# First layer: the row maxima of two heads at once, on the two row halves of the matrix array

## The reference

```python
k_rope = _rotary_apply(c_kv @ W_k_rope, cos, sin)          # 32 rows, shared by all 16 heads
k = (c_kv @ W_k_up).reshape(Bb, Tt, NH, HD)                # 16 heads of 8
q = (x @ W_q).reshape(Bb, Tt, NH, HD)
q_rope = _rotary_apply(x @ W_q_rope, cos, sin)
scores = jnp.einsum('bqhd,bkhd->bhqk', q, k)
scores = scores + jnp.einsum('bqr,bkr->bqk', q_rope, k_rope)[:, None]
scores = jnp.where(causal[None, None], -jnp.inf, scores / scale)
w = jax.nn.softmax(scores, axis=-1)
```

## Time and profile before

| what | us |
|---|---|
| median of three runs | 3255.03 |
| the profiled execution's own time | 3248.36 |
| its span, first to last instruction | 3246.6 |
| PE busy in the span | 3103.6 (96%) |
| DVE busy | 2005.2 (62%) |
| ACT busy | 1632.8 (50%) |
| POOL busy | 1279.7 (39%) |

### The profile page before, as it was taken

One profiled execution on the slowest core, in us unless ns is written; L12 is line 12 of the kernel. 1 busy time (PEld: TensorE's weight loads), 2 busy tenths in 40 slices (PEclk: granted clock), 3 DMA queues, 4 the chain that ended last, 5 costly groups with the idle time before them and its releaser, 6 DMA issues.

```text
span 3246.6 us, 62545 instructions
## 1 busy us (share of the span) xinstructions
PE 3103.6 (96%) x23476; PEld 1674.8 (52%) x23476; DVE 2005.2 (62%) x3829; ACT 1632.8 (50%) x3433; POOL 1279.7 (39%) x1223
## 2 busy tenths in 40 slices
PE   4999999999999994999999999999999999999999
PEld 2565555655555652445555554554554554554554
DVE  5666666656666653666666666666666666666664
ACT  2666656556666663444444444444444444444443
POOL 1333333323333321444444444444444444444444
PEclk9999999999999996999999999999999999999999
DMA  4211122221222113332432432432432442432431
GB/s 116 53 50 50 50 59 63 62 50 50 62 50 52 50 47 107 105 96 76 108 103 71 108 104 71 108 105 70 108 103 72 108 107 68 108 107 68 108 105 43
DMA packets 239643, 259.86 MB, mean 80 GB/s; under 512 B 27248, under 2 KB 228080, under 8 KB 230640
## 3 DMA queue, kind: packets, MB, share of 16 engines
q1 hardware_dynamic: 217680, 239.12, 28.1%
...
## 4 chain that ended last, share of the span: by engine, by line
PE 56%; DVE 2%; DMA 1%; SPq 1%; ACT 1%; POOL 0%; issue 0%; DVEq 0%; POOLq 0%; ACTq 0%
PE l_ps_out L1548 9%; PE l_ps_any L1585 7%; PE l_ps_any L1448 6%; PE l_ps_any L1450 6%; PE l_ps_any L1449 6%; PE l_ps_exp L1531 4%; PE l_ps_exp L1533 4%; PE l_ps_any L1591 3%; PE l_ps_any L1506 3%; PE l_ps_sum L1559 2%; PE l_ps_any L1571 2%; PE l_ps_exp L1535 2%; DMA l_spread<-route_scratch 1%; SPq L1089 1%; PE l_ps_any L1511 1%; PE l_ps_any L1442 1%
## 5 line engine op out<-in xcount | busy, mean ns | idle before, releaser
L1161 POOL TENSOR_TENSOR l_hw<-l_hidden,l_spread 128x512 f32<-128x512 f32 x256 | 325.5, 1277 | 761.5 <-DMA l_spread<-route_scratch 200.2
L614 DVE TENSOR_REDUCE neg_max<-ps_any 128x1 f32<-128x384 f32 (+3 forms) x704 | 417.4, 634 | 269.1 <-PE ps_any L728 264.6
L1249 ACT ACTIVATE l_probs<-l_ps_exp 128x512 f32<-128x512 f32 x640 | 376.9, 596 | 377.4 <-PE l_ps_exp L1535 288.0
L501 ACT ACTIVATE probs<-ps_exp 128x512 f32<-128x512 f32 x640 | 349.3, 602 | 155.2 <-PE ps_exp L743 154.5
L442 POOL TENSOR_SCALAR_AFFINE_SELECT probs<-probs 128x512 f32<-128x512 f32 x256 | 159.4, 634 | 597.4 <-ACT probs L501 597.4
L1370 DVE TENSOR_REDUCE l_neg_max<-l_ps_any 128x2 f32<-128x768 f32 (+2 forms) x384 | 316.4, 863 | 86.4 <-PE l_ps_any L1511 86.0
L1531 PE MATMUL l_ps_exp<-l_q_a,l_k_a 128*128 128x512 f16 (+3 forms) x1024 | 306.4, 300 | 0.3 <-ACT l_probs L1249 0.2
L1548 PE MATMUL l_ps_out<-l_probs,l_v 128*64 128x512 f32 (+3 forms) x2048 | 303.1, 438 | 0.0
L1533 PE MATMUL l_ps_exp<-l_q_b,l_k_b 65*128 65x512 f16 (+3 forms) x1024 | 295.4, 300 | 0.0
L726 PE MATMUL ps_any<-k_st,q_st 120*128 120x128 f16 (+3 forms) x1024 | 252.8, 304 | 36.2 <-DMA k_st<-stack_scratch 35.2
L1256 ACT ACTIVATE l_tanh<-l_ps_any 128x512 f32<-128x512 f32 x272 | 162.4, 597 | 208.2 <-PE l_ps_any L1450 113.7
...
## 6 DMA issues: line engine op xcount, KB each, us to landing
...
l_q_a<-l_q_hi SPq DMA_DIRECT2D x256, 128.0 KB, 2.4
l_q_b<-l_q_lo SPq DMA_DIRECT2D x128, 128.0 KB, 2.4
l_k_a<-l_k_hi SPq DMA_DIRECT2D x128, 128.0 KB, 2.4
l_k_a<-l_k_lo SPq DMA_DIRECT2D x128, 128.0 KB, 2.4
l_k_b<-l_k_hi SPq DMA_DIRECT2D x128, 128.0 KB, 2.4
...
```

The lines of the kernel that those rows point to most:

```text
L501: nc.scalar.activation(probs[:, n % 2, u], ps_exp[:, (10 * g + u) % 3], ACT.Exp, scale=float(HD0 + DR) ** -0.5).then_inc(exp_done.sem, 1)
L614: nc.vector.tensor_reduce(neg_max[:, n % 2, heads[0]:heads[0] + k, t], src, AX.X, ALU.max, negate=True).then_inc(drained["dve"], 1)
L1161: nc.gpsimd.tensor_tensor(dst, hidden[:, k % 2], spread[:, c % 2, n % CHUNK], ALU.mult).then_inc(hw_ok.sem, 1)
L1249: nc.scalar.activation(probs[:, n % 2, u], ps_exp[:, (5 * p + u) % ST_BANKS], ACT.Exp, scale=float(HD1) ** -0.5).then_inc(exp_done.sem, 1)
```

## The change

The group's maxima come from operands of their own, `q_m` and `k_m`: only the high halves, 32 rotary and 8 head rows, for heads 0 and 2 on partitions 0 to 39, for heads 1 and 3 on 64 to 103. `max` has five units as in layer 1: a unit takes one or two blocks `(q, t, c)` (pair of heads, query block, column), puts the two heads side by side on the two row halves into two neighbouring banks, and adds the mask in pieces of 64 columns. SP loads the new operands with 8 more DMAs for groups 0 and 1 of a batch and 4 more for groups 2 and 3, ahead of the old ones. `max` waits for `paired`, and the first `exp` for `stacked`, for which `max` waited until now. The mask is loaded in four pieces. `ORDER0` is a new table.

```diff
-MAX_UNITS = [(0, (0, 1, 2, 3)), (1, (0, 1)), (1, (2, 3))] + [(t, (h,)) for t in (2, 3) for h in range(4)]
+MAX1 = [[(0, 1, 0), (1, 1, 256)], [(0, 2, 0), (0, 0, 384)], [(1, 2, 0), (1, 0, 384)], [(0, 3, 0)], [(1, 3, 0)]]
...
-    ("max", 0, 1, 2), ("max", 0, 1, 3), ("max", 0, 1, 4), ("exp", 0, 0, 3), ("soft_s", 0, 0), ("exp", 0, 0, 4),
+    ("exp", 0, 0, 0), ("exp", 0, 0, 1), ("exp", 0, 0, 2), ("logits_s", 0, 0), ("exp", 0, 0, 3),
...
                     if n <= 1:
                         sp.wait_ge(rot_ok.sem, rot_ok.at(b, 4))
+                        for st, rows in ((q_m, slice(0, DR)), (k_m, slice(DR, 2 * DR))):
+                            for r in range(2):
+                                sp.dma_start(st[HD1 * r:HD1 * r + DR, s],
+                                             rot_hi[rows].unsqueeze(1).to_broadcast([DR, 2, T])
+                                             ).then_inc(paired[s].sem, 16)
+                        sp.wait_ge(scratch_in.sem, scratch_in.at(b, 16 * 6))
+                    for side, st in ((0, q_m), (1, k_m)):
+                        heads = stack_dram[side, G * n:G * n + G, 0:HD0].rearrange("(q r) d t -> r d q t", r=2)
+                        for r in range(2):
+                            sp.dma_start(st[HD1 * r + DR:HD1 * r + DR + HD0, s], heads[r]).then_inc(paired[s].sem, 16)
...
-                    for c, h in enumerate(heads):
-                        out = scores[:, c * w:c * w + w]
-                        pe.matmul(out, q_st[0:K_MAX0, n % 2, h, t * P:t * P + P], k_st[0:K_MAX0, n % 2, h, 0:w],
-                                  start=True, stop=False)
-                        ins = pe.matmul(out[:, t * P:w], ident_h[:], mask_h[:], start=False, stop=True)
+                    scores = [bank(f"max{b}_{n}_{which[1]}{r}") for r in "ab"]
+                    tops = [(r, slice(HD1 * r, HD1 * r + DR + HD0)) for r in range(2)]
+                    for q, t, c in MAX1[which[1]]:
+                        w = (t + 1) * P
+                        for r, rows in tops:
+                            pe.matmul(scores[r][:, c:c + w], q_m[rows, n % 2, q, t * P:t * P + P],
+                                      k_m[rows, n % 2, q, 0:w], start=True, stop=False)
+                        for half in range(2):
+                            to = c + t * P + HD1 * half
+                            for r in range(2):
+                                rows = slice(HD1 * r, HD1 * r + HD1)
+                                ins = pe.matmul(scores[r][:, to:to + HD1], later_h[rows, half], ident_2[rows],
+                                                start=False, stop=(half == 1))
...
+                        ins = nc.vector.tensor_reduce(maxima[:, :, :, 1], scores.rearrange("p r (q k) -> p r q k", q=2),
+                                                      AX.X, ALU.max, negate=True)
+                    else:
+                        for q, t, c in MAX1[u]:
+                            ins = nc.vector.tensor_reduce(maxima[:, :, q, t], scores[:, :, c:c + (t + 1) * P],
+                                                          AX.X, ALU.max, negate=True)
```

More of the change, by code:

```diff
@@ L136 @@
[L136 to L160, removed]
@@ L161 @@
-    ("load_heads", 1, 1), ("turn_max", 1, 0), ("max", 1, 1, 0), ("out", 0, 0), ("exp", 1, 0, 0),
-    ("exp", 1, 0, 1), ("exp", 1, 0, 2), ("max", 1, 1, 1),
+    ("exp", 0, 0, 0), ("exp", 0, 0, 1), ("exp", 0, 0, 2), ("logits_s", 0, 0), ("exp", 0, 0, 3),
+    ("soft_s", 0, 0), ("logits_s", 0, 1), ("exp", 0, 0, 4), ("share_s", 0, 0), ("soft_s", 0, 1),
+    ("share_s", 0, 1), ("max", 0, 1, 3), ("exp", 0, 0, 5), ("logits_s", 0, 2), ("exp", 0, 0, 6),
+    ("exp", 0, 0, 7), ("soft_s", 0, 2), ("logits_s", 0, 3), ("exp", 0, 0, 8), ("soft_s", 0, 3),
@@ new lines @@
+    ("exp", 0, 0, 9), ("values", 0, 0, 0), ("max", 0, 1, 4), ("turn_max", 0, 1), ("load", 1, 0),
+    ("share_s", 0, 2), ("load_heads", 0, 3), ("share_s", 0, 3), ("values", 0, 0, 1), ("outT", -1, 0),
+    ("max", 0, 2, 0), ("max", 0, 2, 1), ("exp", 0, 1, 0), ("max", 0, 2, 2), ("exp", 0, 1, 1), ("exp", 0, 1, 2),
+    ("dispatch", 0, 0), ("dispatch", 0, 1), ("exp", 0, 1, 3), ("exp", 0, 1, 4), ("exp", 0, 1, 5),
+    ("max", 0, 2, 3), ("logits_c", 0, 0), ("norm", 1, 0), ("dispatch", 0, 2), ("share_c", 0, 0),
@@ new lines @@
+    ("soft_c", 0, 0), ("exp", 0, 1, 6), ("dispatch", 0, 3), ("slots", 0, 0), ("exp", 0, 1, 7), ("exp", 0, 1, 8),
+    ("max", 0, 2, 4), ("logits_c", 0, 1), ("values", 0, 0, 2), ("soft_c", 0, 1), ("out_rows", 0, 0),
+    ("exp", 0, 1, 9), ("hidden", 0, 0), ("turn_max", 0, 2), ("hidden", 0, 1), ("hidden", 0, 2),
+    ("values", 0, 1, 0), ("hidden", 0, 3), ("scale", 1, 0), ("exp", 0, 2, 0), ("exp", 0, 2, 1),
+    ("square", 1, 0), ("max", 0, 3, 0), ("values", 0, 1, 1), ("out_rows", 0, 1), ("turn_rows", 0, 0),
@@ new lines @@
+    ("max", 0, 3, 1), ("max", 0, 3, 2), ("values", 0, 1, 2), ("max", 0, 3, 3), ("exp", 0, 2, 2),
+    ("exp", 0, 2, 3), ("exp", 0, 2, 4), ("logits_c", 0, 2), ("exp", 0, 2, 5), ("max", 0, 3, 4),
+    ("soft_c", 0, 2), ("xnT", 1, 0), ("values", 0, 2, 0), ("exp", 0, 2, 6), ("share_c", 0, 1),
+    ("share_c", 0, 2), ("turn_max", 0, 3), ("low_q", 1, 0), ("ckv", 1, 0), ("exp", 0, 2, 7), ("q", 1, 0),
+    ("exp", 0, 2, 8), ("exp", 0, 2, 9), ("k", 1, 0), ("low_k", 1, 0), ("r", 1, 0), ("soft_c", 0, 3),
@@ new lines @@
+    ("logits_c", 0, 3), ("values", 0, 2, 1), ("exp", 0, 3, 0), ("xf", 1, 0), ("exp", 0, 3, 1), ("exp", 0, 3, 2),
+    ("values", 0, 2, 2), ("expert_out", 0, 0), ("exp", 0, 3, 3), ("exp", 0, 3, 4), ("out_rows", 0, 2),
+    ("turn_rows", 0, 1), ("exp", 0, 3, 5), ("xfT", 1, 0), ("exp", 0, 3, 6), ("values", 0, 3, 0),
+    ("share_c", 0, 3), ("exp", 0, 3, 7), ("combine", 0, 0), ("max", 1, 0, 0), ("max", 1, 0, 1),
+    ("exp", 0, 3, 8), ("exp", 0, 3, 9), ("combine", 0, 1), ("out_rows", 0, 3), ("turn_rows", 0, 2),
@@ L163 @@
+    ("values", 0, 3, 1), ("max", 1, 0, 2), ("values", 0, 3, 2), ("load_heads", 1, 0), ("combine", 0, 2),
+    ("max", 1, 0, 3), ("turn_rows", 0, 3), ("v", 1, 0), ("max", 1, 0, 4), ("combine", 0, 3), ("attnT", 0, 0),
+    ("load_heads", 1, 1), ("turn_max", 1, 0), ("max", 1, 1, 0), ("out", 0, 0), ("load_heads", 1, 2),
+    ("max", 1, 1, 1), ("max", 1, 1, 2),
 )
@@ L306, in layer0 @@
         stacked = [sig(f"stacked{s}", 16 * 10) for s in range(2)]
+        paired = [sig(f"paired{s}", 16 * 12) for s in range(2)]
         row_in = sig("row_in", 16)
@@ L355, in layer0 @@
                  (w_v[:], a["L0_attn_W_v_up"]), (w_o[:], a["L0_attn_W_o"])] + rope
+        loads += [(mask[HD1 * r:HD1 * r + HD1, half], a["maskT"][HD1 * half:HD1 * half + HD1])
+                  for r in range(2) for half in range(2)]
         late_loads = [(b1[:], a["L0_ffn_b1"]),
```

53 lines of the change are left out of this document (26 added, 27 removed).

## The result

The changed kernel takes 3263.66 us (median of 7 runs, 3259.81 to 3267.63) against 3252.64 us (7 runs on the same chip, 3251.52 to 3259.85) before: ratio 1.0034, 95% interval 1.0024 to 1.0043. It is slower by a third of a per cent, and the forecast was 3227, faster. The profiled execution took 3262.89 us, 14.5 more than that of before.

A forecast was written before the change was run, and what follows sets the result against it. PE was taken to bound the kernel. Per batch: -6.2 stream, +1.2 shape, +7.1 - 1.75 banks, +0.8 - 3.0 DMAs, so -1.85 us; -30 over sixteen batches, +2 at the start: 3227 us, range 3165 to 3262.

The forecast's parts named there:

- What bounds the kernel: Layer 0: PE, busy 96% of the span, is a packed queue; about 4.7 us of a 74.3 us batch are waits.
- What comes to PE: Paired maxima units in layer 0, priced from layer 1's same shapes: 1.61 us of PE per group.
- rival 3: Paired maxima of layer 0: halves do not run side by side at 40 rows; 3262 us, chance 0.04.
- What goes from PE: Old maxima units of layer 0: 3.15 us of PE per group removed; net saving 6.2 us per batch.
- What the change of shape costs: Borders of maxima bunches on PE: 13 of 32 pay 0.09 us each, 1.2 us per batch.
- What DVE does, the 7.1: Refills behind paired maxima in layer 0: PE waits for banks not yet emptied, 7.1 us per batch.
- Rival 1: Layer 0's banks come free in time and most stream is gained; 3142 us, or 3185 with half the waits; chance 0.25.
- What DVE does, the -1.75: Old maxima's weight loading waits for DVE to return a bank; 1.75 us per batch counted as removed.
- What SP does: DMA issues per batch rise from 32 to 56; PE's waits for DMA fall from 3.0 to 0.8 us per batch.
- rival 2: SP's DMA issuing becomes the bound at group 1 of the next batch; slower, 3281 us at 0.72 us per issue; chance 0.11.
- the credit: The 1.75 us per batch of old bank waits for DVE at the maxima, subtracted in the forecast's sum.

The follow-up runs named there:

- full height: Changed kernel with one full-height 128-row product of both heads' sum and one 128-wide mask product into one bank: 3242.78 us, ratio 0.9966.

## Why the prediction was wrong

- **What bounds the kernel**: right. PE's queue does, and the waits that replaced those for DMA are waits of PE.
- **What comes to PE**: right. The paired units cost 6.4 us per batch, as predicted (4 x 1.61), and 40 rows pair as 64 do; rival 3 is refuted.
- **What goes from PE**: right. The old maxima take 12.8 us a batch, 12.6 were predicted; the stream saved is 6.4 us instead of 6.2.
- **What the change of shape costs**: the price of a border was right (0.09, measured 0.10), the count was not: I let 13 of 32 pay and called the others hidden. 27 pay, 2.45 us instead of 1.2, since a border beside a wait or beside another bunch's refill is not hidden by it. The old bunches had 0.93 at their own borders, which I had not counted, so the term comes to +1.5. What it costs the time is less again, for a border also gives the readers time: 1.4 came back with full height.
- **What DVE does, the 7.1**: right in size and mechanism, and the size partly by luck. By the distances between starts the waits for banks are 7.05 us per batch: `turn_max` 1.56 against 1.5, group 0's chain 1.6 against 1.8, unit 2 behind `out` 0.56 against 0.55, but `combine` 1 0.2 against 0.7, group 2 0.8 against 1.2, group 3 0.7 against 1.1. Not in my list were the refills in front of a pair that wait for copies: `outT`'s addition (`x`, 0.70) and `combine` 0 (`disp_n`, 0.47); nor `values` behind `y_un` (0.37). Too much at some places and nothing at others gave the right sum. Rival 1 is refuted.
- **What DVE does, the -1.75**: the step that failed most. I took 28.1 us for which the weight load of the old maxima stood idle, 1.75 per batch, as time of PE that DVE costs now and that the change would give back. PE itself has no such wait in its batches before. With short reductions in the kernel before, DVE is named for 15 us less, but the weight load stands idle as long and the time falls by 2. So nothing came back: +7.05 instead of +5.35, the upper end of my own bounds, and 1.7 of the 2.0 us by which the sum was off. The short reductions in both kernels show that it is the paired units, in the table that came with them, that make DVE's time count: 49 us here, 2 before.
- **What SP does**: right. The waits for DMA went by 2.6 per batch (2.2 predicted); rival 2 is refuted by the rows and by sending the row from ACT.
- **Everything else**: counted at nothing, it is 0.6 us per batch longer. What makes it is open.
- **The end of layer 0**: counted at nothing, it cost 5.9 us. 2.7 of them are a wait of `values` for POOL that the kernel before does not have there, and behind it the clock stands at 0.5 for 3.4 us, 1.7 us of time.

The misses are 1.7 for the credit, 0.3 of shape and 0.6 of the rest, less 0.2 of stream and 0.4 of DMA: 2.0 us per batch, and -1.85 became +0.14 in these fourteen batches. The sum of terms as large as 7 us each was off by 2, and 2 is what it had to decide. The range's upper end, 3262, was drawn for one rival at a time; that the credit could be worth nothing while the borders cost more was not in it. And a clock that falls, as in three of the experiments, has no place in such a sum at all.
